# First layer norm: the normalisation moved from VectorE to ScalarE, one tile in each of four steps

## The chip, the cores and the metric

One core of a Trainium2 chip. The metric is the device time of the kernel in microseconds (us), median of the runs shown.

## What is computed

Four sequences of 2048 rows with 256 values each go through an attention and a layer norm, then through a mixture of 32 experts and a second layer norm:

```python
Q, K, V = sign(x * sign(bq)), sign(x * sign(bk)), x * sign(bv)
scores  = einsum('btd,bsd->bts', Q, K) / 16           # causal
x1      = layernorm(x + einsum('bts,bsd->btd', where(causal, sigmoid(4 * scores), 0), V))
probs   = softmax(x1 @ w_router);  top1 = argmax(probs);  gate = probs[top1]
# rows go to the slots of their expert, 320 slots for each; rows over that stay alone
y       = (silu(buf @ w_gate[e]) * (buf @ w_up[e])) @ w_down[e]
out     = layernorm(x1 + gate * y)
```

## The kernel before

The first stage is attention with routing. For each of the four batches b, 40 steps k run over tiles of scores: the rows are taken in four groups g of four tiles (512 rows, GT = 4), and group g takes 4g+4 steps, so that the groups end at steps 3, 11, 23 and 39. The last steps of a group cover 512, 384, 256 and 128 columns. In step k:

- TensorE computes scores(k+2) (L716, L719), then values(k): up to twelve matmuls (L738 to L740), three for each of the four tiles of the group. It is L738 that waits for the two inputs.
- ScalarE computes weights(k): the sigmoid of the scores twice, into a_ring (L572) and, rounded, into the high half of hl_ring (L574). 
- VectorE computes low(k): the difference of the two (L929), the low half of hl_ring. values(k) needs it.

Between these, each engine does the work of the finished groups at steps that tables at the head of the file give. A group's chain is: VectorE adds the residual and takes row statistics (SUM, STATS; L935, L941, L949); GpSimd works out the reciprocal standard deviation with two `pow` operations (rstd, L378 to L388, of which L380 gives the factor that the normalisation needs); VectorE normalises the four tiles into xrow (NORM, L957); TensorE transposes them (TURN, L757), ScalarE copies the transposed rows (COPY, L581), TensorE computes the logits (L765), VectorE picks the expert (L967 to L983), ScalarE computes two sigmoids for the gate (EXPS, L587, L588), VectorE works out the slot and the gate (PLACE, GATE; L1023 is the gate's last operation), and GpSimd scatters the four tiles to the expert buffers with four indirect DMAs (L409). GpSimd also computes rows_alone, the output of rows without an expert, from xrow (L395), and for the next rows the signed values (L357) and their low part (L364). ScalarE computes their high part (VHIGH, L555), the signs (SIGN, L547) and the keys (KEY, L561).

Each engine works through its instructions in the order in which the program lists them: a wait holds up everything behind it on that engine. GpSimd's order within a batch, n being 4b, is rstd and rows_alone of group 3 of the batch before; rstd(n), values_signed(b, 2), values_low(b, 2), rows_alone(n), scatter(n-1), rstd(n+1), values_signed(b, 3), rows_alone(n+1), scatter(n), rstd(n+2), values_low(b, 3), values_signed(b+1, 0), rows_alone(n+2), scatter(n+1), values_low(b+1, 0), values_signed(b+1, 1), scatter(n+2), values_low(b+1, 1). In the first batch there is no group before.

The normalisation of group 3 falls into steps 3 and 4 of the next batch; that of the last batch comes after the loop. The groups' tiles lie in two buffers, res (even groups) and xs (odd groups); xrow has two halves as well, and a half is written again only when the scatter of the group before in it has landed. The second stage, the experts, follows the first and isn't touched by the change.

Of the kernel before, what the change touches and what calls it, by code (L numbers as in the profile page):

```python
# [17 lines left out]
ALU = mybir.AluOpType  # L18
ACT = mybir.ActivationFunctionType
# [12 lines left out]
GT = 4  # L32
# [7 lines left out]
SUM = {0: (2, 3, 4, 4), 1: (10, 11, 12, 12), 2: (22, 23, 24, 24),  # L40
       3: (38, 39, 40, 40)}
STATS = {3: 1, 0: 6, 1: 15, 2: 26}
NORM = {3: (3, 4), 0: (13, 13), 1: (21, 21), 2: (29, 29)}
TURN = {3: 4, 0: 13, 1: 21, 2: 29}
COPY = {3: 6, 0: 15, 1: 23, 2: 31}
ROUTE = {3: 6, 0: 15, 1: 23, 2: 31}
# [13 lines left out]
def bass_postln_attn_moe_kernel(nc, x, bv_q, bv_k, bv_v, w_router, w_gate, w_up, w_down, out):  # L60
    B, T, D = x.shape
    E, _, F = w_gate.shape
    NT = B * T // P
    NG = T // GQ
# [21 lines left out]
    with ExitStack() as ctx:  # L86
# [15 lines left out]
        mone = sb("mone", [P, GT], F32)  # L102
# [16 lines left out]
        mv = sb("mv", [P, GT, 2], F32)  # L119
        small = sb("small", [P, 8, GT], F32)  # L120
        xrow = sb("xrow", [P, 2, GT, ROW], F32)
# [33 lines left out]
        res = (res_even, res_odd)  # L155
# [31 lines left out]
        mv_ready = sem("mv_ready")  # L187
        rstd_step = sem("rstd_step")
        x1_ready = sem("x1_ready")
# [17 lines left out]
        scattered = [sem(f"scattered{i}") for i in range(2)]  # L207
# [23 lines left out]
        def atleast(eng, s, value, settle=False):  # L231

            if isinstance(value, int) and value <= 0:
                return
            if settle and not isinstance(value, int):
                value = eng.to_reg(value)
                eng.wait_ge(consts, 10)
            eng.wait_ge(s, value)  # L240

        block = ctx.enter_context(nc.Block())
        M0, M1 = 6, 7

        def cols(k):
# [78 lines left out]
        def _(pool):  # L324
            g_ = nc.gpsimd
# [38 lines left out]
                g_.tensor_tensor(v_hl[:, 1, sl, :], v_f32, v_hl[:, 0, sl, :].bitcast(F32), ALU.subtract)\  # L364
                    .then_inc(v_ready, 1)

            RN = 6

            def rstd(G, par):


                atleast(pool, mv_ready, (G + 1) * GT, settle=True)

                atleast(pool, alone_ready, G, settle=True)
                base = G * RN
                atleast(pool, x1_ready, G * GT, settle=True)
                var = mv[:, :, 1]
                g_.tensor_scalar(small[:, 0, :], var, EPS, None, ALU.add).then_inc(rstd_step, 1)  # L378
                atleast(pool, rstd_step, base + 1, settle=True)
                g_.tensor_tensor(small[:, 1, :], small[:, 0, :], mhalf[:, :], ALU.pow).then_inc(rstd_step, 1)  # L380
                atleast(pool, rstd_step, base + 2, settle=True)
                g_.tensor_tensor(small[:, 2, :], var, small[:, 1, :], ALU.mult).then_inc(rstd_step, 1)
                atleast(pool, rstd_step, base + 3, settle=True)
                g_.tensor_tensor(small[:, 3, :], small[:, 2, :], small[:, 1, :], ALU.mult).then_inc(rstd_step, 1)
                atleast(pool, rstd_step, base + 4, settle=True)
                g_.tensor_scalar(small[:, 4, :], small[:, 3, :], EPS / 4, None, ALU.add).then_inc(rstd_step, 1)
                atleast(pool, rstd_step, base + 5, settle=True)
                g_.tensor_tensor(small[:, 5, :], small[:, 4, :], mhalf[:, :], ALU.pow).then_inc(rstd_step, 1)  # L388

            def rows_alone(G, half, par):  # L390
# [141 lines left out]
        def _(act):  # L532
            s_ = nc.scalar
# [43 lines left out]
            def copy_x1t(G):  # L577
                act.wait_ge(x1_turned, G + 1)
                atleast(act, logits_done, G)
                for c in range(DC):  # L580
                    s_.activation(x1_t[:, c, :], ps[:, M0 + c, :], ACT.Copy).then_inc(x1t_ready, 1)  # L581

            def gates(G):

                act.wait_ge(below_ready, G + 1)
                atleast(act, gate_ready, G)
                s_.activation(sg[:, 0, :, :], below[:, :, :], ACT.Sigmoid).then_inc(sg_ready, 1)  # L587
                s_.activation(sg[:, 1, :, :], below[:, :, :], ACT.Sigmoid, scale=-1.0).then_inc(sg_ready, 1)  # L588
# [10 lines left out]
            def batch(b, first, last):  # L599
                for k in range(NS):  # L600
                    weights(b, k)
                    for g in (3, 0, 1, 2):
                        if g == 3 and first:
                            continue
                        bb = b - 1 if g == 3 else b
                        if k == COPY[g]:
                            copy_x1t(bb * NG + g)
                        if k == EXPS[g]:
                            gates(bb * NG + g)
                    if first and k == 3:  # L610
                        values_high(0, 1)
                    for q in range(NG):
                        for c in range(DC):
                            if k == KEY[q][c] and not (q == 0 and last):
                                keys(b + 1 if q == 0 else b, q, c)
                        if q in AHEAD and last:
                            continue
                        bb = b + 1 if q in AHEAD else b
                        if k == SIGN[q]:
                            signs(bb, q)  # L620
                        if k == VHIGH[q]:
                            values_high(bb, q)
                    if last and k in (NS - 4, NS - 2):

                        act.wait_ge(pv_done, (B - 1) * NS + OFF[3] + 2 * GT)
                        high_weights(0, (k - NS + 4) // 2)
# [8 lines left out]
            with act.Fori(1, B - 1) as b:  # L635
                batch(b, False, False)
            batch(B - 1, False, True)
            copy_x1t(B * NG - 1)
            gates(B * NG - 1)
            act.wait_ge(table_ready, 1)  # L640
# [265 lines left out]
        def _(dve):  # L906
            v_ = nc.vector
# [24 lines left out]
            def residual(G, i, done, par):  # L932

                dve.wait_ge(pv_done, done)
                v_.tensor_tensor(res[par][:, i, :], ps[:, 2 + i, 0:D], xall[:, G * GT + i, :], ALU.add)\  # L935
                    .then_inc(res_ready, 1)

# [5 lines left out]
            def statistics(G, par):  # L943

                row_statistics(G, GT - 1, par)
                dve.wait_ge(stats_step, (G + 1) * GT)
                atleast(dve, rstd_step, G * 6, settle=True)
                for i in range(GT):
                    v_.bn_aggr(mv[:, i, :], stats[:, par, i, :]).then_inc(mv_ready, 1)  # L949

            def normalise(G, turn, par, tiles=range(GT)):
                dve.wait_ge(rstd_step, G * 6 + 2)
                dve.wait_ge(mv_ready, (G + 1) * GT)

                atleast(dve, scattered[par], turn * 16 * GT)
                for i in tiles:
                    v_.tensor_scalar(xrow[:, par, i, 0:D], res[par][:, i, :], mv[:, i, 0:1], small[:, 1, i:i + 1],  # L957
                                     ALU.subtract, ALU.mult).then_inc(x1_ready, 1)

            SN = 13  # L960

# [75 lines left out]
            def batch(b, first, last):  # L1037
                for k in range(NS):
                    low(b, k)
                    for g in range(NG):  # L1040
                        for i in range(GT):
                            if k == SUM[g][i]:
                                add_tile(b, g, i)
                            if k + NS == SUM[g][i] and not first:
                                add_tile(b - 1, g, i)
                    for g in (3, 0, 1, 2):
                        if g == 3 and first:
                            continue
                        G = (b - 1 if g == 3 else b) * NG + g
                        turn = 2 * b + {3: -1, 0: 0, 1: 0, 2: 1}[g]  # L1050
                        if k == STATS[g]:
                            statistics(G, g % 2)
                        for half in range(2):
                            if k == NORM[g][half]:
                                normalise(G, turn, g % 2, range(half * GT // 2, (half + 1) * GT // 2))
                        if k in (PICK[g], PICK[g] + 1):
                            pick(G, k - PICK[g])
                        if k == PLACE[g]:
                            place(G, g % 2)
                        for part in range(2):  # L1060
                            if k == GATE[g][part]:
                                gate(G, g % 2, part)
                    for q in range(NG):
                        if k == QUERY[q] and not (q in AHEAD and last):
                            queries(b + 1 if q in AHEAD else b, q)
# [11 lines left out]
            G = B * NG - 1  # L1077
# [1 line left out]
            add_tile(B - 1, 3, 3)  # L1079
            statistics(G, 1)  # L1080
            low_weights(0, 0)
            normalise(G, 2 * B - 1, 1)
            low_weights(0, 1)
            pick(G, 0)
            pick(G, 1)
# [97 lines left out]
```

## Time and profile before

| | |
|---|---|
| median of 3 runs | 687.56 us (684.07 to 689.95) |
| span of the profiled execution, first to last instruction | 678.2 us |
| first stage in it | to about 400 us |
| TensorE matmul busy | 604.2 us, 89% |
| mean granted TensorE clock | 0.965 |

Where the engines are in each batch, from the timeline (us; a step's number in brackets):

| batch | weights(3) ends | L380 of group 3 ends | weights(18) ends | L380 of group 1 ends | weights(28) ends | L380 of group 2 ends |
|---|---|---|---|---|---|---|
| 0 | | | 51.25 | 47.59 | 71.41 | 72.63 |
| 1 | 107.09 | 110.57 | 145.52 | 149.80 | 166.02 | 167.24 |
| 2 | 204.16 | 206.81 | 241.66 | 245.95 | 262.16 | 263.45 |
| 3 | 297.43 | 300.86 | 334.65 | 338.76 | 354.72 | 355.52 |

An undisturbed full step, from the start of values(k) to that of values(k+1), takes TensorE 1.87 us, the eight transposes of a group 0.87 us more.

The profile shows for each engine when an instruction ran and what ended the idle time before it. A matmul's record is longer than the distance to the next one, since matmuls are pipelined.

### The profile page before, as it was taken

The page shows a single profiled execution, that of the slowest core. Times are in us where ns is not written, and L with a number is a line of the kernel's source. Part 1 is how long each engine was busy: PE and PEld are TensorE (multiplying, and loading weights), DVE is VectorE, ACT ScalarE, POOL GpSimd, SP SyncE. Part 2 cuts the span into 40 slices and gives each one's busy share as a digit, 9 for nine tenths or more (in the row PEclk, how much of TensorE's full clock was granted, in tenths as well). Part 3 has the DMA queues.
Part 4 walks back from the last instruction along what each step waited for, and adds up shares of the span by engine and source line. Part 5 has one row for each costly group of instructions (what it writes and reads, how often), then busy time and mean ns, then how long its engine had stood idle before and what let it go on. Part 6 is the DMA issues. An engine that isn't in the chain of part 4 may idle for free.

```text
span 678.2 us, 14737 instructions
## 1 busy us (share of the span) xinstructions
PE 604.2 (89%) x4175; PEld 504.3 (74%) x4214; DVE 485.0 (72%) x1300; ACT 353.4 (52%) x678; POOL 415.3 (61%) x547
## 2 busy tenths in 40 slices
PE   5989898899879898988999879999999999999960
PEld 4878787698768687876888637877788778878750
DVE  2669978879787989698898624666776677766740
ACT  5566566456455655666555312555445554555520
POOL 4563757467857377765576520566666666676773
PEclk9999999999999899899999998999999999999995
DMA  8962021132201112206111020566555565566300
GB/s 273 368 211 78 32 80 59 37 96 94 94 29 62 50 39 93 86 23 219 58 59 49 31 87 28 148 193 187 169 158 176 171 190 168 159 184 195 118 32 21
DMA packets 68206, 78.11 MB, mean 115 GB/s; under 512 B 7934, under 2 KB 59374, under 8 KB 68160
## 3 DMA queue, kind: packets, MB, share of 16 engines
q1 hardware_dynamic: 60992, 63.26, 30.1%
q0 software_dynamic: 7168, 14.30, 5.9%
q8 instruction: 21, 0.34, 0.2%
q14 instruction: 25, 0.20, 0.1%
HBM read 44.29 MB, written 37.90 MB: 121 GB/s over the span
## 4 chain that ended last, share of the span: by engine, by line
PE 68%; DVE 9%; issue 8%; ACT 6%; POOL 5%; DMA 2%; SPq 0%; ACTq 0%; DVEq 0%; POOLq 0%
PE ps L877 13%; PE ps L738 8%; PE ps L739 6%; PE ps L740 6%; PE ps L862 6%; PE ps L864 5%; PE ps L863 5%; PE ps L716 5%; PE ps L846 5%; PE ps L765 4%; DVE hl_ring L929 4%; DVE xrow L957 2%; PE ps L757 2%; ACT hl_ring L574 2%; POOL out_dram L490 2%
## 5 line engine op out<-in xcount | busy, mean ns | idle before, releaser
L738 PE MATMUL ps<-v_hl,hl_ring 128*128 128x256 f32 x544 | 176.6, 325 | 25.6 <-DVE hl_ring L929 16.7
L739 PE MATMUL ps<-v_hl,hl_ring 128*128 128x256 f32 x544 | 156.0, 287 | 0.0
L740 PE MATMUL ps<-v_hl,hl_ring 128*128 128x256 f32 x544 | 155.6, 286 | 0.0
L738 PEld LDWEIGHTS ps<-v_hl,hl_ring 128*128 128x128 f32 x544 | 105.9, 195 | 51.5 <-issue 28.4
L490 POOL DMA_INDIRECT out_dram<-alone,ids x96 | 108.0, 1125 | 55.8 <-ACT alone L665 22.5
L572 ACT ACTIVATE a_ring<-ps 128x512 f32<-128x512 f32 (+3 forms) x160 | 85.7, 535 | 91.1 <-PE ps L716 49.9
L929 DVE TENSOR_TENSOR hl_ring<-a_ring,hl_ring 128x512 fp32r<-128x512 f32 (+3 forms) x160 | 119.1, 748 | 19.0 <-ACT hl_ring L574 8.8
L409 POOL DMA_INDIRECT expert_rows<-xrow,slot x64 | 68.7, 1074 | 63.9 <-issue 26.1
L739 PEld LDWEIGHTS ps<-v_hl,hl_ring 128*128 128x128 f32 x544 | 106.2, 195 | 1.9
L740 PEld LDWEIGHTS ps<-v_hl,hl_ring 128*128 128x128 f32 x544 | 106.0, 195 | 0.0
L877 PE MATMUL ps<-xall,a_ring 128*128 128x256 f32 (+1 forms) x384 | 95.9, 392 | 1.1 <-DVE a_ring L1107 1.1
L574 ACT ACTIVATE hl_ring<-ps 128x512 fp32r<-128x512 f32 (+3 forms) x160 | 85.9, 537 | 0.0
L862 PE MATMUL ps<-hl_ring,v_hl 128*128 128x320 f32 x256 | 83.3, 325 | 0.0
L716 PE MATMUL ps<-q_t,k_t 128*128 128x512 bf16 (+3 forms) x284 | 79.9, 354 | 3.3 <-ACT hl_ring L574 1.3
L656 ACT ACTIVATE a_ring<-ps 128x320 f32<-128x320 f32 x64 | 28.0, 437 | 103.8 <-PE ps L864 103.8
L864 PE MATMUL ps<-hl_ring,v_hl 128*128 128x320 f32 x256 | 79.4, 310 | 0.0
L863 PE MATMUL ps<-hl_ring,v_hl 128*128 128x320 f32 x256 | 79.3, 310 | 0.0
L877 PEld LDWEIGHTS ps<-xall,a_ring 128*128 128x128 f32 (+1 forms) x384 | 60.9, 171 | 24.0 <-issue 10.6
L1107 DVE TENSOR_TENSOR a_ring<-a_ring,ps 128x320 f32<-128x320 f32 x64 | 31.2, 488 | 56.4 <-ACT a_ring L656 56.4
L395 POOL TENSOR_TENSOR alone<-xrow,small 128x1024 f32<-128x1024 f32 x16 | 33.8, 2112 | 42.2 <-DVE xrow L957 31.9
L862 PEld LDWEIGHTS ps<-hl_ring,v_hl 128*128 128x128 f32 x256 | 48.4, 189 | 12.4 <-issue 12.2
L665 ACT ACTIVATE alone<-z,zrs 128x256 f32<-128x256 f32 (+1 forms) x96 | 50.3, 588 | 9.4 <-POOL zrs L481 9.4
(108 smaller groups left out, 1125.3 us busy)
## 6 DMA issues: line engine op xcount, KB each, us to landing
expert_rows<-xs SPq DMA_DIRECT2D x40, 258.0 KB, 5.6
xs<-expert_rows SPq DMA_DIRECT2D x32, 258.0 KB, 3.0
xall<-in_L_attn_x_dram SPq DMA_DIRECT2D x16, 512.0 KB, 4.1
out_dram<-alone SPq DMA_DIRECT2D x16, 512.0 KB, 3.1
xall<-in_L_ffn_w_gate_dram SPq DMA_DIRECT2D x32, 256.0 KB, 3.6
xall<-in_L_ffn_w_up_dram SPq DMA_DIRECT2D x32, 256.0 KB, 3.9
xall<-in_L_ffn_w_down_dram SPq DMA_DIRECT2D x32, 256.0 KB, 4.2
xs<-expert_rows SPq DMA_DIRECT2D x32, 64.5 KB, 3.0
```

What stands on the lines that cost most here:

```text
L490: g_.indirect_dma_start(out=out_rows, out_offset=bass.IndirectOffsetOnAxis(ap=ids[0:rows, n % U, t:t + 1], axis=0), in_=o_s[0:rows, p, t, ...
L572: s_.activation(a_ring[:, r, lo:GQ], ps[:, k % 2, lo:GQ], ACT.Sigmoid, scale=0.25)\
L574: s_.activation(hl_ring[:, 0, r, lo:GQ], ps[:, k % 2, lo:GQ], ACT.Sigmoid, scale=0.25)\
L716: last = mm(o, k_t[:, c, j * P:(j + 1) * P], q_t[:, c, g * GQ + lo:(g + 1) * GQ], start=(c == 0), stop=(c == DC - 1 and not diag))
L738: mm(o, ah, v_hl[:, 0, j, :], start=(j == 0), stop=False)
L739: mm(o, ah, v_hl[:, 1, j, :], start=False, stop=False)
L740: last = mm(o, al, v_hl[:, 0, j, :], start=False, stop=(j == GT * g + i))
L862: mm(o, wh, x_h[:, p, c, :], start=(c == 0), stop=False)
L863: mm(o, wh, x_l[:, p, c, :], start=False, stop=False)
L864: last = mm(o, wl, x_h[:, p, c, :], start=False, stop=(c == DC - 1))
L877: last = mm(o, act_h[:, p, f, t * P:t * P + m], raw[:, s, 4 + f, :], start=(f == 0), stop=(f == FC - 1))
L929: v_.tensor_tensor(hl_ring[:, 1, r, lo:GQ], a_ring[:, r, lo:GQ], hl_ring[:, 0, r, lo:GQ].bitcast(F32), ALU.subtract).then_inc(al_ready, 1)
```

## The change

- The four VectorE operations (L957) that subtract the mean and multiply by the reciprocal standard deviation are gone. ScalarE computes `scale * x + bias` instead, with bias = -mean * rstd.
- For that GpSimd's rstd has two more operations: -mean, ahead of the first pow, and its product with rstd, behind it. A group has now eight steps of `rstd_step` (RN = 8), and the normalisation waits for the fourth, where it waited for the second.
- NORM gives a step for each tile. ScalarE does a tile's normalisation right behind weights(k), ahead of its other work of that step. Group 0 begins at step 10 (before: 13), group 1 at 18 (21), group 2 at 28 (29), group 3 at 3 (3).
- residual waits for the normalisation two groups before, whose buffer it writes (it was VectorE's own order before).

```diff
-NORM = {3: (3, 4), 0: (13, 13), 1: (21, 21), 2: (29, 29)}
+NORM = {3: (3, 3, 4, 4), 0: (10, 11, 12, 13), 1: (18, 19, 20, 21), 2: (28, 28, 29, 29)}
@@ rstd, GpSimd
                 g_.tensor_scalar(small[:, 0, :], var, EPS, None, ALU.add).then_inc(rstd_step, 1)
-                atleast(pool, rstd_step, base + 1, settle=True)
+                g_.tensor_tensor(small[:, 6, :], mv[:, :, 0], mone[:, :], ALU.mult).then_inc(rstd_step, 1)
+                atleast(pool, rstd_step, base + 2, settle=True)
                 g_.tensor_tensor(small[:, 1, :], small[:, 0, :], mhalf[:, :], ALU.pow).then_inc(rstd_step, 1)
-                atleast(pool, rstd_step, base + 2, settle=True)
+                atleast(pool, rstd_step, base + 3, settle=True)
+                g_.tensor_tensor(small[:, 7, :], small[:, 6, :], small[:, 1, :], ALU.mult).then_inc(rstd_step, 1)
@@ ScalarE
+            def normalise(G, turn, par, tiles=range(GT)):
+                act.wait_ge(rstd_step, G * RN + 4)
+                atleast(act, scattered[par], turn * 16 * GT)
+                for i in tiles:
+                    s_.activation(xrow[:, par, i, 0:D], res[par][:, i, :], ACT.Identity,
+                                  bias=small[:, 7, i:i + 1], scale=small[:, 1, i:i + 1]).then_inc(x1_ready, 1)
@@ ScalarE, batch, behind weights(b, k)
+                        for i in range(GT):
+                            if k == NORM[g][i]:
+                                normalise(bb * NG + g, turn, g % 2, range(i, i + 1))
@@ VectorE, residual
                 dve.wait_ge(pv_done, done)
+                atleast(dve, x1_ready, (G - 1) * GT)
@@ VectorE
-            def normalise(G, turn, par, tiles=range(GT)):
-                dve.wait_ge(rstd_step, G * 6 + 2)
-                dve.wait_ge(mv_ready, (G + 1) * GT)
-                atleast(dve, scattered[par], turn * 16 * GT)
-                for i in tiles:
-                    v_.tensor_scalar(xrow[:, par, i, 0:D], res[par][:, i, :], mv[:, i, 0:1], small[:, 1, i:i + 1],
-                                     ALU.subtract, ALU.mult).then_inc(x1_ready, 1)
```

## Rows read from the trace of the kernel before

**Rows 1.** Groups by line and shape (busy, mean, idle before), then L957 alone (min/median/max).

```profile
L957 DVE TENSOR_SCALAR xrow<-res,mv,small 128x256 f32<-128x256 f32 x32 | 25.8, 866 | 0.0
L957 DVE TENSOR_SCALAR xrow<-xs,mv,small 128x256 f32<-128x256 f32 x32 | 17.6, 604 | 1.9 <-POOL small L380 1.9
L957 DVE TENSOR_SCALAR xrow<-res,mv,small x32: 399/407/2593, 41.0 to 361.0; 128x256 f32<-128x256 f32 x32
```

**Rows 2.** Waits of TensorE, 22 to 400 us: total, times, longest.

```profile
PE ps L738 <- DVE hl_ring L929: 15.4, 19, 2.0
PE ps L757 <- DVE xrow L957: 7.5, 4, 2.0
```

**Rows 3.** Timeline of batch 1 around step 18: start, duration, idle before.

```profile
144.93 0.59 ACT L574 ACTIVATE hl_ring<-ps 128x512 fp32r<-128x512 f32 x1
146.53 0.31 ACT L587 ACTIVATE sg<-below 128x128 f32<-128x128 f32 x1 [1.01 <-DVE below L974]
146.63 1.33 POOL L409 DMA_INDIRECT expert_rows<-xrow,slot  x1 [0.30 <-issue]
146.95 0.58 ACT L572 ACTIVATE a_ring<-ps 128x512 f32<-128x512 f32 x1
148.52 1.28 POOL L380 TENSOR_TENSOR small<-small,mhalf 128x4 f32<-128x4 f32 x1
150.24 0.36 PE L738 MATMUL ps<-v_hl,hl_ring 128*128 128x256 f32 x1
```

**Rows 4.** Timeline: three ScalarE affine operations and one small GpSimd one, second stage.

```profile
504.06 1.57 ACT L665 ACTIVATE alone<-z,zrs 128x256 f32<-128x256 f32 x3
479.77 0.20 POOL L481 TENSOR_TENSOR zrs<-zrs 128x3 f32<-128x3 f32 x1
```

**Rows 5.** Timeline of batch 2, steps 3 and 4.

```profile
203.89 0.27 ACT L574 ACTIVATE hl_ring<-ps 128x128 fp32r<-128x128 f32 x1
206.97 0.73 DVE L957 TENSOR_SCALAR xrow<-xs,mv,small 128x256 f32<-128x256 f32 x2 [0.42 <-POOL small L380]
208.54 0.38 PE L738 MATMUL ps<-v_hl,hl_ring 128*128 128x256 f32 x1 [0.60 <-DVE hl_ring L929]
```

**Rows 6.** Timeline of batch 1, steps 28 to 30.

```profile
165.43 0.59 ACT L574 ACTIVATE hl_ring<-ps 128x512 fp32r<-128x512 f32 x1
166.20 1.04 POOL L380 TENSOR_TENSOR small<-small,mhalf 128x4 f32<-128x4 f32 x1
167.16 0.60 ACT L572 ACTIVATE a_ring<-ps 128x512 f32<-128x512 f32 x1 [0.20 <-PE ps L716]
169.56 5.48 DVE L957 TENSOR_SCALAR xrow<-res,mv,small 128x256 f32<-128x256 f32 x4
169.80 2.41 POOL L364 TENSOR_TENSOR v_hl<-z,v_hl 128x1024 fp32r<-128x1024 f32 x1
172.46 2.42 POOL L357 TENSOR_TENSOR z<-xall,bv_row 128x1024 f32<-128x1024 f32 x1 [0.25 <-POOL v_hl L364]
175.09 0.44 PE L757 MATMUL ps<-ident,xrow 128*128 128x128 f32 x2 [1.91 <-DVE xrow L957]
175.78 0.36 PE L738 MATMUL ps<-v_hl,hl_ring 128*128 128x256 f32 x1
```

**Rows 7.** Timeline of batch 1, steps 10 and 11.

```profile
126.81 2.36 POOL L364 TENSOR_TENSOR v_hl<-z,v_hl 128x1024 fp32r<-128x1024 f32 x1 [2.33 <-ACT v_hl L555]
127.08 2.24 DVE L929 TENSOR_TENSOR hl_ring<-a_ring,hl_ring 128x128 fp32r<-128x128 f32 x1
```

**Rows 8.** Busy time by window (us, instructions): PE, PEld, DVE, ACT, POOL; granted clock, DMA.

```profile
130.00:132.00 2.00, 0.51 (x3) 0.01 (x1) 1.93 (x9) 2.00 (x4) 0.00 (x0) 1.00 0.00 0
132.00:134.00 2.00, 1.91 (x11) 1.92 (x12) 2.00 (x6) 0.07 (x1) 0.00 (x0) 0.65 0.00 0
134.00:136.00 2.00, 2.00 (x9) 1.54 (x9) 2.00 (x6) 0.47 (x1) 0.64 (x1) 0.50 0.00 0
```

**Rows 9.** Timeline of the end of the first stage.

```profile
384.14 1.38 DVE L957 TENSOR_SCALAR xrow<-xs,mv,small 128x256 f32<-128x256 f32 x4 [1.24 <-POOL small L380]
386.06 1.08 ACT L581 ACTIVATE x_t<-ps 128x512 f32<-128x512 f32 x2 [7.82 <-PE ps L757]
```

More of the change, by code:

```diff
@@ L242, in bass_postln_attn_moe_kernel @@
         block = ctx.enter_context(nc.Block())
+        RN = 8
         M0, M1 = 6, 7
@@ L365, in values_low @@
                     .then_inc(v_ready, 1)
-            RN = 6
             def rstd(G, par):
@@ L378, in rstd @@
                 g_.tensor_scalar(small[:, 0, :], var, EPS, None, ALU.add).then_inc(rstd_step, 1)
-                atleast(pool, rstd_step, base + 1, settle=True)
+                g_.tensor_tensor(small[:, 6, :], mv[:, :, 0], mone[:, :], ALU.mult).then_inc(rstd_step, 1)
+                atleast(pool, rstd_step, base + 2, settle=True)
                 g_.tensor_tensor(small[:, 1, :], small[:, 0, :], mhalf[:, :], ALU.pow).then_inc(rstd_step, 1)
-                atleast(pool, rstd_step, base + 2, settle=True)
+                atleast(pool, rstd_step, base + 3, settle=True)
+                g_.tensor_tensor(small[:, 7, :], small[:, 6, :], small[:, 1, :], ALU.mult).then_inc(rstd_step, 1)
                 g_.tensor_tensor(small[:, 2, :], var, small[:, 1, :], ALU.mult).then_inc(rstd_step, 1)
-                atleast(pool, rstd_step, base + 3, settle=True)
+                atleast(pool, rstd_step, base + 5, settle=True)
                 g_.tensor_tensor(small[:, 3, :], small[:, 2, :], small[:, 1, :], ALU.mult).then_inc(rstd_step, 1)
-                atleast(pool, rstd_step, base + 4, settle=True)
+                atleast(pool, rstd_step, base + 6, settle=True)
                 g_.tensor_scalar(small[:, 4, :], small[:, 3, :], EPS / 4, None, ALU.add).then_inc(rstd_step, 1)
-                atleast(pool, rstd_step, base + 5, settle=True)
+                atleast(pool, rstd_step, base + 7, settle=True)
                 g_.tensor_tensor(small[:, 5, :], small[:, 4, :], mhalf[:, :], ALU.pow).then_inc(rstd_step, 1)
@@ L605, in batch @@
                         bb = b - 1 if g == 3 else b
+                        turn = 2 * b + {3: -1, 0: 0, 1: 0, 2: 1}[g]
+                        for i in range(GT):
+                            if k == NORM[g][i]:
+                                normalise(bb * NG + g, turn, g % 2, range(i, i + 1))
                         if k == COPY[g]:
@@ L637, in _ @@
             batch(B - 1, False, True)
+            normalise(B * NG - 1, 2 * B - 1, 1)
             copy_x1t(B * NG - 1)
@@ L946, in statistics @@
                 dve.wait_ge(stats_step, (G + 1) * GT)
-                atleast(dve, rstd_step, G * 6, settle=True)
+                atleast(dve, rstd_step, G * RN, settle=True)
                 for i in range(GT):
                     v_.bn_aggr(mv[:, i, :], stats[:, par, i, :]).then_inc(mv_ready, 1)
-            def normalise(G, turn, par, tiles=range(GT)):
-                dve.wait_ge(rstd_step, G * 6 + 2)
-                dve.wait_ge(mv_ready, (G + 1) * GT)
-                atleast(dve, scattered[par], turn * 16 * GT)
-                for i in tiles:
-                    v_.tensor_scalar(xrow[:, par, i, 0:D], res[par][:, i, :], mv[:, i, 0:1], small[:, 1, i:i + 1],
-                                     ALU.subtract, ALU.mult).then_inc(x1_ready, 1)
             SN = 13
@@ L1049, in batch @@
                         G = (b - 1 if g == 3 else b) * NG + g
-                        turn = 2 * b + {3: -1, 0: 0, 1: 0, 2: 1}[g]
                         if k == STATS[g]:
                             statistics(G, g % 2)
-                        for half in range(2):
-                            if k == NORM[g][half]:
-                                normalise(G, turn, g % 2, range(half * GT // 2, (half + 1) * GT // 2))
                         if k in (PICK[g], PICK[g] + 1):
@@ L1081, in _ @@
             low_weights(0, 0)
-            normalise(G, 2 * B - 1, 1)
             low_weights(0, 1)
```

## The prediction

> **What bounds the kernel now.** Only the first stage, to about 400 us, is touched. I read the waits of TensorE in it first, then the groups of instructions by line, then the timeline step by step, noting for each of the 160 steps when weights, low and values started.
>
> TensorE is the bound where it isn't waiting, and most of its waits end with a VectorE operation: 15.4 us for the low halves and 7.5 us, four times about 1.9, for the normalised rows [rows 2]. The normalisation takes 43.4 us of VectorE though one operation, undisturbed, takes 0.407 us, or 26.0 us for 64; the 17.4 us above that are blocking [rows 1]. The reader sees it at step 29: the four operations take 5.48 us while GpSimd runs L364 and L357 under them, TensorE waits 1.91 us, and values(30) starts at 175.78, where 1.87 for values(29) and 0.87 for the transposes behind its start at 170.52 would give about 173.3 [rows 6]. So VectorE looks overloaded, and ScalarE idle for long times. But the wait that I looked for next is another: when is the factor ready that the normalisation needs, and where is ScalarE then in its own program?
>
> **What is removed.** 43.4 us of VectorE, 26.0 of them work. On TensorE's path that is at most the 7.5 us.
>
> **What is added on ScalarE.** 64 affine operations with a scale and a bias for each row. The same shape and form runs in the second stage: three in 1.57 us [rows 4], one alone 0.59, so each further one costs (1.57 - 0.59) / 2 = 0.49 us of the engine, 31 us in all, 1.96 for a group. ScalarE is some 0.8 us idle in a full step of 1.87 us, so the work alone fits. Its bound is 0.49 from below and 0.59 from above; I take 0.49, since they stand in a queue of others.
>
> **What is added on GpSimd.** Two small operations, 0.20 us each by the nearest row [rows 4], the second behind a semaphore: L380 ends, and 0.14 us later the next begins. The factor and the bias are there 0.25 + 0.35 = 0.6 us later than the pow's end in before. From below it is 0.4 (no gap), from above 0.9 (L382 takes up to 0.44).
>
> **The wait, group by group.** On ScalarE it holds back weights of the next steps, which low and then values wait for.
>
> *Group 1, steps 18 to 21.* In batch 1, weights(18) ends at 145.52. The factor comes from L380, which ends at 149.80, since it stands in GpSimd's order behind the scatter of four tiles, whose last starts at 146.63, and that waits for a gate of step 16 [rows 3]. With the 0.6 us ScalarE stands still till 150.4, 4.9 us, where VectorE came to this only at 152.34. Then: one tile 0.49, the gates 0.42 (146.53 to 146.95), weights(19) 1.06, low 0.69 and 0.2 for the semaphores: values(19) starts at 153.3, for 150.24 [rows 3]. That is 3.0 us of TensorE. Steps 20 and 21 carry a tile and a key each (0.49 + 0.72 + 0.96 = 2.2 us for a step of 1.87), 0.3 us more; some 0.3 us of waiting at steps 22 and 23, where GpSimd's L395 blocks low, goes away. Sum 3.0 us. Batches 2 and 3 repeat it (weights(18) ends 241.66 and 334.65, L380 at 245.95 and 338.76); in batch 0 there is no scatter ahead, and the factor is early. 3 x 3.0 = 9.0 us. The scatter into this half of xrow must also have landed; a landing takes 2.7 us from 146.63 to 147.96, so it comes at 149.3 to 150.7, with the factor.
>
> *Group 3, steps 3 and 4 of the next batch.* In batch 2, weights(3) ends at 204.16. The factor came at 206.81, VectorE waited for it too (0.42) and needed 0.73 for two tiles; values(4) started at 208.54 [rows 5]. Now ScalarE waits till 207.4, does two tiles (208.4) and only then weights(4), which was done at 207.10 before: 209.5, low 210.2, values(4) 210.3. That is 1.8 us; ScalarE then has two tiles and a key before weights(5) and two more operations before weights(6), and with rows_alone blocking low(5) I get 2.2 at values(5) and 2.0 at values(6). Batches 1 and 3 look the same (ScalarE would wait 4.1 and 4.0 us). 3 x 2.0 = 6.0 us.
>
> *Group 2, steps 28 and 29.* Weights(28) ends at 166.02, the factor is there at 167.24 + 0.6 = 167.85, a wait of 1.8 us (the same in all four batches, 1.4 to 1.9). Two tiles and the signs (1.0) move the start of weights(29) from 167.16 [rows 6] to 169.8, its end to 170.8. By then L364, 0.45 us later for the two new operations, runs from 170.3 to 172.7, then L357 [rows 6]. The question is whether low, which takes the place of the normalisation on VectorE, is blocked as it was. It is an operation on two tiles in SBUF, and at step 11 one of 0.28 us takes 2.24 us under L364, whose end it waits for [rows 7]. So low(29) runs at 172.7, low(30) at 175.7, values(30) starts at 176.5, for 175.78: the stall isn't taken away but moved, and 0.7 us are lost. Batch 0 gives 0.3, batch 3 between 0 and 2.1, taken as 1. Sum 2.7 us.
>
> The Trainium skill says in "SBUF — State Buffer", Who interferes with whom, that a VectorE instruction with two SBUF inputs contends with a GpSimd instruction that reads SBUF, and not only the two-port modes do. By a reading in which only the two-port modes block, the three stalls of about 2.5 us at step 30 would go and the sum would be some 8 us lower; the trace agrees with the page's wider rule, by the 2.24 us.
>
> *Group 0, steps 10 to 13.* The factor is early. A tile ahead of L555 moves L364, which waits for it, by 0.49 us, and with it the end of the blocked low(11) [rows 7]: 0.5 us in batches 1 to 3, 1.5 us. The 1.4 us that VectorE saves at step 13 are given to no wait: TensorE has none behind it.
>
> *The end.* Behind the last batch nothing covers the chain. VectorE's four tiles start at 384.14 and take 1.38; ScalarE starts 0.6 later and takes 3 x 0.49 + 0.59 = 2.06; the copies at 386.06 [rows 9] move by up to 1.3 us. TensorE transposes tile by tile: 1.0 us.
>
> The new wait of residual costs nothing: the group two before was normalised at least 17 steps earlier.
>
> **Sum.** 9.0 + 6.0 + 2.7 + 1.5 + 1.0 = 20.2 us on a span of 678.2. The median of the runs is 687.6, 9.4 above the span, and I carry the difference over: 707.8, rounded to 708 us.
>
> **The rivals.**
>
> *More: the clock.* After waits of 1.3, 1.6 us and others in the same few us, TensorE's granted clock is 0.65 and then 0.50, its lower level of 1.2 GHz, from about 132.6 to 136 us [rows 8]; five such stretches of 3.4 us lie in the first stage, each worth 1.7 us. One wait of 1.9 us by itself, at 175, brought none. Each of my six stalls of 2 to 3 us could bring one: 6 x 1.7 = 10 us, 718 us. For it: the stalls of 2.0 us at 200 and at 80 did. Against it: the stalls at 174 didn't, and some of the five old ones may go.
>
> *About the same: the delay is given back.* VectorE has 26 us less to do, and the 15.4 us of waits for low [rows 2] are partly its own queue at steps 0 to 12 and 34. If 12 of them went, the sum would be 8 us, 696; with an earlier factor (scatter shorter, GpSimd ahead) it would be within 1%. Against it: most of these waits end when a GpSimd operation ends, as at step 11 [rows 7], and that order isn't changed. About 690.
>
> *Faster: the relief counts.* ScalarE's waits are covered and VectorE's 7.5 us for the rows go, with two of the stretches at the lower clock (3.4 us): 687.6 - 10.9 = 677 us. It decides at step 18: weights(19) must start by 148.3, so the factor must be there by 147.4, 3 us earlier than the rows give it [rows 3]. The Trainium skill says in "Perfetto Trace Analysis", Optimizing Scalar/DVE Operations, that offloading work to ScalarE may make sense where VectorE is saturated; VectorE's share here bears that out, the order of the waits doesn't.
>
> **How the numbers follow.** The forecast 0.60, more by the clock 0.18, given back 0.13, faster 0.09. Slower by over 1% is then 0.78, within 1% 0.12, faster 0.10; 1%, 6.9 us, is about what a measurement of this kernel can tell from no change. The range leaves out the faster case and the half of the third that lies lowest: from 692 (a third of the sum left) to 718 (the clock in full).
>
> **What would show it.** In the profile after: ScalarE's operation on xrow waits for GpSimd's small tile, some 3 to 5 us, six times, at steps 3 and 18; waits of TensorE for ScalarE's or VectorE's hl_ring grow by 15 to 20 us and those for xrow vanish; low operations of 2 to 3 us appear at steps 29 and 30. I am wrong if ScalarE's waits for the small tile stay below 10 us in all, or if they are there and TensorE's idle time in the first stage doesn't grow.

## The result: 4% slower, and the profile after

| | before | after |
|---|---|---|
| median of 5 runs each | 687.83 us (684.07 to 693.30) | 717.38 us (711.29 to 718.86) |
| ratio, 95% interval | | 1.0399 [1.034, 1.0458] |
| again, beside the experiments | 689.37 us (13 runs) | 714.37 us (4 runs), 1.0365 [1.0295, 1.0434] |
| span of the profiled execution | 678.2 us | 709.5 us |
| mean granted TensorE clock in it | 0.965 | 0.959 |

Ratios, here and below, compare the faster executions of each kernel with each other; medians are over all of them. The forecast was 708 us, from 692 to 718: slower, and the time is in the range, 0.6 us from its upper end. The change costs 29.5 us between the medians and 31.3 us between the spans, where 20.2 us were forecast.

First the engines' busy time in the profile of after:

```profile
PE 610.3 (86%) x4175; PEld 508.6 (72%) x4214; DVE 459.4 (65%) x1236; ACT 382.3 (54%) x742; POOL 416.9 (59%) x579
```

VectorE is busy 25.6 us less than before (485.0 there), ScalarE 28.9 us more (353.4 there). The work went where it was sent, ScalarE is still idle almost half of the time, and the kernel is slower: shares of busy time say nothing here. The waits do. TensorE's and ScalarE's in the first stage of after, 22 to 425 us (total, times, longest):

```profile
PE ps L752 <- DVE hl_ring L943: 30.5, 32, 2.2
PE ps L730 <- ACT hl_ring L575: 16.9, 10, 3.6
PE ps L752 <- ACT hl_ring L575: 6.0, 5, 1.3
PE ps L771 <- ACT xrow L589: 3.3, 1, 3.3
```

```profile
ACT xrow L589 <- POOL small L382: 39.6, 11, 7.3
```

The second fence is the cause, as the experiments below bear out, the first its effect. ScalarE's normalisation (L589) waits for GpSimd's bias (L382) eleven times. One of them, 7.3 us, is at the end of the stage, where ScalarE has nothing else to do; the ten others are 32.3 us in the middle of the loop. TensorE waits 30.5 us for low (L943; the answering row was 15.4 us in [rows 2]) and 22.9 us for ScalarE's weights (8.4 us in before), most of it in front of the next scores (L730), since ScalarE hadn't read the old ones. Together these waits grew by 29.6 us, for the 15 to 20 us that the forecast named. The four waits for xrow of [rows 2], 7.5 us, are down to the one at the end.

The timeline of batch 1 around step 18, answering to [rows 3] (start, duration, idle before):

```profile
151.64 0.59 ACT L575 ACTIVATE hl_ring<-ps 128x512 fp32r<-128x512 f32 x1
153.24 0.31 ACT L596 ACTIVATE sg<-below 128x128 f32<-128x128 f32 x1 [1.00 <-DVE below L981]
153.65 1.01 POOL L410 DMA_INDIRECT expert_rows<-xrow,slot  x1 [0.30 <-issue]
155.40 1.04 POOL L380 TENSOR_TENSOR small<-small,mhalf 128x4 f32<-128x4 f32 x1
156.59 0.20 POOL L382 TENSOR_TENSOR small<-small 128x4 f32<-128x4 f32 x1
156.82 0.60 ACT L589 ACTIVATE xrow<-xs,small 128x256 f32<-128x256 f32 x1 [3.07 <-POOL small L382]
157.33 0.58 ACT L573 ACTIVATE a_ring<-ps 128x512 f32<-128x512 f32 x1
158.48 0.69 DVE L943 TENSOR_TENSOR hl_ring<-a_ring,hl_ring 128x512 fp32r<-128x512 f32 x1 [3.46 <-ACT hl_ring L575]
158.82 2.59 POOL L358 TENSOR_TENSOR z<-xall,bv_row 128x1024 f32<-128x1024 f32 x1
160.07 1.49 DVE L1022 TENSOR_TENSOR quot<-quot,sg 128x128 f32<-128x128 f32 x1
161.48 0.68 DVE L943 TENSOR_TENSOR hl_ring<-a_ring,hl_ring 128x512 fp32r<-128x512 f32 x1
163.12 1.89 POOL L396 TENSOR_TENSOR alone<-xrow,small 128x1024 f32<-128x1024 f32 x1 [1.71 <-ACT xrow L589]
163.13 1.90 DVE L1013 SCALAR_TENSOR_TENSOR slot<-rt 128x4 uint32<-128x4 f32 x1
164.96 0.88 DVE L943 TENSOR_TENSOR hl_ring<-a_ring,hl_ring 128x384 fp32r<-128x384 f32 x2
```

Weights(18) ends at 152.23. The gates (L596, L597) come at 153.24 to 153.75, and then ScalarE stands still until L382 ends at 156.79: the factor is 4.56 us behind weights(18). Weights(19), the next line of the program, can't start before 157.33, and low(19) waits for it on an idle VectorE (3.46 us). So far that is the forecast. The second half of the fence is not in it: GpSimd's L358 and L396 now lie over small operations of the gate on VectorE, L1022 (1.49 us) and L1013 (1.90 us), and low(20) and low(21) stand behind these.

Group 2, batch 1, steps 28 to 30, answering to [rows 6]:

```profile
177.81 0.53 POOL L377 TENSOR_SCALAR small<-mv 128x4 f32<-128x4 f32 x1 [4.98 <-issue]
180.24 1.10 ACT L589 ACTIVATE xrow<-res,small 128x256 f32<-128x256 f32 x2 [2.81 <-POOL small L382]
182.16 2.35 POOL L365 TENSOR_TENSOR v_hl<-z,v_hl 128x1024 fp32r<-128x1024 f32 x1
182.19 0.57 ACT L573 ACTIVATE a_ring<-ps 128x512 f32<-128x512 f32 x1
183.34 1.72 DVE L943 TENSOR_TENSOR hl_ring<-a_ring,hl_ring 128x512 fp32r<-128x512 f32 x1 [2.16 <-ACT hl_ring L575]
184.76 2.54 POOL L358 TENSOR_TENSOR z<-xall,bv_row 128x1024 f32<-128x1024 f32 x1 [0.25 <-POOL v_hl L365]
185.29 2.56 DVE L943 TENSOR_TENSOR hl_ring<-a_ring,hl_ring 128x512 fp32r<-128x512 f32 x1 [0.23 <-ACT hl_ring L575]
```

ScalarE waits again, 2.81 us. Low(29) and low(30), 0.69 us when undisturbed, take 1.72 and 2.56 us under L365 and L358; each ends 0.55 us behind the end of the GpSimd operation over it. The blocking that the normalisation suffered in [rows 6] has moved onto low. Over the whole stage VectorE's group of low shows it (busy, mean ns, idle before and its releasers); before, this group was busy 115.2 us, mean 742 ns:

```profile
L943 DVE TENSOR_TENSOR hl_ring<-a_ring,hl_ring 128x512 fp32r<-128x512 f32 (+3 forms) x156 | 127.2, 820 | 73.0 <-ACT a_ring L573 38.2 <-ACT hl_ring L575 31.8 <-issue 1.7
```

Low is busy 12.0 us longer for the same 156 operations; in before the normalisation was blocked for 17.4 us.

**Where the 31.3 us lie.** From the start of values at the ends of the stretches, after minus before, summed over the batches (where four numbers follow, they are batches 0 to 3):

| stretch of steps | group at work | forecast | measured |
|---|---|---|---|
| 34 of the batch before to 9 (step 3) | 3 | 6.0 | 7.8 |
| 9 to 18 (step 10) | 0 | 1.5 | 0.5 |
| 18 to 25 (step 18) | 1 | 9.0 | 12.05: 0, 4.04, 4.02, 4.00 |
| 25 to 34 (step 28) | 2 | 2.7 | 9.6: 4.66, 1.48, 1.49, 1.96 |
| end of the stage | 3 of the last batch | 1.0 | 1.4 |

### The profile page after: what moved, and what is told of

Read it like the earlier page. It is cut to its first block, busy times and chain, and to the rows that moved or that the text cites. A ratio compares the mean times of both kernels' runs of the same rounds, so it can differ in the third digit from the quotient of the medians.

```text
span 709.5 us, 14839 instructions
## 1 busy us (share of the span) xinstructions
PE 610.3 (86%) x4175; PEld 508.6 (72%) x4214; DVE 459.4 (65%) x1236; ACT 382.3 (54%) x742; POOL 416.9 (59%) x579
## 4 chain that ended last, share of the span: by engine, by line
PE 52%; issue 15%; ACT 10%; DVE 10%; POOL 9%; DMA 1%; ACTq 1%; POOLq 0%; DVEq 0%; SPq 0%
PE ps L891 12%; PE ps L876 6%; DVE hl_ring L943 6%; PE ps L878 5%; PE ps L877 5%; PE ps L860 5%; PE ps L752 4%; PE ps L754 3%; PE ps L753 3%; POOL expert_rows L410 3%; ACT a_ring L573 3%; PE ps L779 3%; ACT hl_ring L575 2%; PE ps L730 2%; PE ps L771 2%
## 5 line engine op out<-in xcount | busy, mean ns | idle before, releaser
L943 DVE TENSOR_TENSOR hl_ring<-a_ring,hl_ring 128x512 fp32r<-128x512 f32 (+3 forms) x160 | 131.1, 824 | 73.0 <-ACT a_ring L573 38.2
L410 POOL DMA_INDIRECT expert_rows<-xrow,slot x64 | 66.8, 1044 | 88.2 <-issue 47.8
L730 PE MATMUL ps<-q_t,k_t 128*128 128x512 bf16 (+3 forms) x284 | 80.5, 356 | 21.0 <-ACT hl_ring L575 17.3
L396 POOL TENSOR_TENSOR alone<-xrow,small 128x1024 f32<-128x1024 f32 x16 | 32.7, 2042 | 28.6 <-ACT xrow L589 22.7
```

The source lines that it names most:

```text
L730: last = mm(o, k_t[:, c, j * P:(j + 1) * P], q_t[:, c, g * GQ + lo:(g + 1) * GQ], start=(c == 0), stop=(c == DC - 1 and not diag))
L943: v_.tensor_tensor(hl_ring[:, 1, r, lo:GQ], a_ring[:, r, lo:GQ], hl_ring[:, 0, r, lo:GQ].bitcast(F32), ALU.subtract).then_inc(al_ready, 1)
```

## The experiments

The theory: the price is ScalarE standing still in its own order for a factor that GpSimd has ready only later. The rivals: the 31 us of added work on ScalarE; the two added operations on GpSimd; the clock. A difference from one experiment to the next is read together with the granted clock, since the kernel before alone runs from 681.5 to 699.4 us, most of it with its clock. "Clock-free" is a rough correction: the median of time minus span x (1 - granted clock) over all executions, this kernel minus before on the same chip. A single execution of before lies some 2.3 us around its median by this measure. It can take off too much: in after, batch 1 has a stretch at the lower clock behind step 18 and batch 2 has none, and both lose the same 4.0 us there.

| run | median / before | ratio [95%] | clock-free |
|---|---|---|---|
| e1_waits_only | 696.60 / 691.16 | 1.0128 [1.007, 1.0185] | +7.1 |
| e2_work_only | 695.63 / 691.16 | 1.005 [1.0011, 1.009] | +1.3 |
| e3_pool_only | 684.91 / 691.16 | 0.9919 [0.9886, 0.9953] | -0.9 |
| e4_g1_late | 704.12 / 691.16 | 1.0151 [1.0064, 1.0239] | +12.7 |
| e5_wait_and_work | 700.14 / 689.37 | 1.0181 [1.0119, 1.0242] | +10.5 |
| e6_all_late | 690.26 / 689.37 | 1.0026 [0.9992, 1.006] | +3.1 |
| e7_g0_only | 693.88 / 689.37 | 1.0109 [1.0029, 1.0188] | -0.2 |
| after_again | 714.37 / 689.37 | 1.0365 [1.0295, 1.0434] | +23.9 |
| e8_g2_late_only | 682.85 / 690.30 | 0.992 [0.9886, 0.9953] | -4.3 |
| e9_wait_work_pool | 712.32 / 690.30 | 1.0334 [1.0286, 1.0382] | +12.0 |

**e1: the waits alone.** The kernel before, ScalarE waits for the factor and does nothing with it:

```diff
+            HOLD = {3: 3, 1: 18, 2: 28}
+                        if k == HOLD.get(g):
+                            act.wait_ge(rstd_step, (bb * NG + g) * 6 + 2)
```

> The kernel before, VectorE normalises as it did; ScalarE does no new work, but waits at steps 3, 18 and 28, where the changed kernel's normalisation begins, for GpSimd's factor of that group. Theory of the wait (what costs is that ScalarE's queue stands still until GpSimd has the factor, 4.6 us at step 18 in the trace after): 12 to 22 us slower than before. Rival of the work (what costs is 64 times 0.49 us on ScalarE, 31 us, which happens to be the whole difference): the same as before, within 3 us.

A wait that guards nothing costs 1.3%, 7.1 us without the clock: more than the rival's 3 us, less than the 12 to 22 us expected. In its profile ScalarE waits 10.3 + 3.6 us for GpSimd's factor, and the steps 17 to 25 of batch 1 take 18.86 us, where they take 16.76 in before and 20.80 in after. So the wait is a cause, about a third of the whole by this run (its factor comes from before's shorter chain).

**e2: the work alone.** The kernel before, with ScalarE operations of the same shape and number at the new steps, without a wait. Their rows are extra work that nobody reads.

```diff
+EXTRA = {3: (3, 3, 4, 4), 0: (10, 11, 12, 13), 1: (18, 19, 20, 21), 2: (28, 28, 29, 29)}
+                        for i in range(GT):
+                            if k == EXTRA[g][i]:
+                                s_.activation(idle[:, i, :], bv_row[:, :], ACT.Identity, bias=mone[:, i:i + 1],
+                                              scale=mhalf[:, i:i + 1])
```

> The kernel before, VectorE normalises as it did; ScalarE does at each of the new steps one affine operation of the same shape and form, from a constant row into a tile that nobody reads, without a wait. Theory of the wait: 1 to 8 us slower than before, since a full step leaves ScalarE 0.8 us. Rival of the work: 25 to 31 us slower.

0.5%, 1.3 us of it left without the clock, for 64 operations that take 31 us of the engine. That is in the 1 to 8 us expected. The rival of the work falls: ScalarE had the room.

**e3: the two GpSimd operations alone.** Before with after's rstd; VectorE waits for step 4 of rstd_step and normalises as it did.

> The kernel before with GpSimd's two new small operations of each group, and VectorE's normalisation waits for the second of them. ScalarE has nothing new. Theory of the wait: 0 to 3 us slower, 0.45 us in each of the places where GpSimd is late. A rival, that GpSimd's longer chain is what delays everything behind it: 7 us (16 times 0.45) or more.

Not slower, as 0 to 3 us had been expected, but 0.8% faster: 6.3 us between the medians, of which the clock-free time leaves 0.9 us. The longer chain costs nothing where ScalarE doesn't stand waiting for it. Why the clock was higher in this kernel (median 0.963, before 0.956) isn't shown.

**e4: group 1 three steps later.** The kernel after, with one entry changed:

```diff
-NORM = {3: (3, 3, 4, 4), 0: (10, 11, 12, 13), 1: (18, 19, 20, 21), 2: (28, 28, 29, 29)}
+NORM = {3: (3, 3, 4, 4), 0: (10, 11, 12, 13), 1: (21, 21, 22, 22), 2: (28, 28, 29, 29)}
```

> The changed kernel with one number pattern changed: group 1 is normalised at steps 21, 21, 22, 22 instead of 18, 19, 20, 21, when the factor is there. Theory of the wait: of the 12 us that the trace after shows between steps 18 and 25 some 9 to 12 go, 18 to 23 us over before. Rival of the work: nothing changes, 29 us over before, or more since two tiles stand in one step.

The ratio falls from 1.0365 to 1.0151, the clock-free loss from 23.9 to 12.7 us (13.0 us between the medians, less than the 18 to 23 expected). In its profile ScalarE waits eight times for L382, where it waited eleven times, and the stretch of steps 18 to 25 loses 2.65 us, for 12.05. The work and where it is done are after's; the place of one group in ScalarE's program alone is worth 11 us, clock-free. Its waits:

```profile
ACT xrow L589 <- POOL small L382: 28.1, 8, 7.3
```

**e5: wait and work.** e2, with ScalarE waiting for before's factor in front of its first extra operation of a group (the extra rows are again read by nobody).

> Both halves together in the kernel before: ScalarE waits for GpSimd's factor at the first step of each group and does one affine operation in each of the four places, on rows that nobody reads; VectorE still normalises. If wait and work were priced apart, the sum of the two runs before this: 9 + 3 = 12 us slower than before. If they multiply (what the wait leaves behind, a queue with no slack, meets a step that is 0.2 us too long for ScalarE), 20 to 30 us, and nothing of the change's price has to do with VectorE.

1.0181, against 1.0128 and 1.005 for the two alone: they add up, as the first of the two expectations had it, and make not quite half of the clock-free loss of after (10.5 of 23.9 us).

**e6: everything late.** The kernel after, with each group at a step where its factor is ready; for group 0 that is where it was:

```diff
-NORM = {3: (3, 3, 4, 4), 0: (10, 11, 12, 13), 1: (18, 19, 20, 21), 2: (28, 28, 29, 29)}
+NORM = {3: (5, 5, 6, 6), 0: (10, 11, 12, 13), 1: (21, 21, 22, 22), 2: (29, 29, 30, 30)}
-TURN = {3: 4, 0: 13, 1: 21, 2: 29}
+TURN = {3: 5, 0: 13, 1: 22, 2: 30}
```

> The changed kernel with ScalarE's normalisation at steps at which the factor is there: group 3 at 5, 5, 6, 6, group 1 at 21, 21, 22, 22, group 2 at 29, 29, 30, 30, and the transposes of these groups one step later (5, 22, 30). Theory of the wait: at most 10 us over before, since work alone cost 3 and the end 1. Rival of the work: 25 us or more. If 12 to 20 us, late rows cost what the early wait did.

1.0026: nearly the whole loss is gone, with all 64 tiles on ScalarE and the two operations on GpSimd. ScalarE's waits in its profile, of which 7.3 us are the harmless one at the end:

```profile
ACT xrow L589 <- POOL small L382: 8.7, 4, 7.3
```

And its steps 29 and 30 of batch 1:

```profile
174.12 1.09 ACT L589 ACTIVATE xrow<-res,small 128x256 f32<-128x256 f32 x2 [0.61 <-POOL small L382]
175.12 0.58 ACT L573 ACTIVATE a_ring<-ps 128x512 f32<-128x512 f32 x1
176.05 2.39 POOL L365 TENSOR_TENSOR v_hl<-z,v_hl 128x1024 fp32r<-128x1024 f32 x1
176.27 2.72 DVE L943 TENSOR_TENSOR hl_ring<-a_ring,hl_ring 128x512 fp32r<-128x512 f32 x1 [0.47 <-ACT hl_ring L575]
178.69 2.54 POOL L358 TENSOR_TENSOR z<-xall,bv_row 128x1024 f32<-128x1024 f32 x1 [0.25 <-POOL v_hl L365]
179.43 1.82 DVE L1030 TENSOR_SCALAR xrow<-rt 128x4 f32<-128x4 f32 x1
```

Low(29) is through before L365 starts; only low(30) is blocked (2.72 us), and under L358 lies no low but the gate's last operation. Steps 25 to 34 take 21.91 us, where they take 25.14 in before and 26.62 in after.

**e7: group 0 alone on ScalarE**, at steps 10 to 13; the other groups on VectorE as before, with after's rstd (VectorE waits for its third step).

> Only group 0, whose factor is early, is normalised on ScalarE at steps 10 to 13; groups 1, 2 and 3 are normalised on VectorE at the steps of before. Theory of the wait: within 3 us of before, a quarter of the work is moved and none of the waits. Rival of the work: a quarter of 30 us, 7 us slower. If moving work off VectorE helps where nothing waits, faster by up to 3 us.

Slower by 1.1% with an interval from 0.3 to 1.9%, over four executions, and nothing of it left without the clock (-0.2 us). By the ratio alone the rival's 7 us would fit, by the clock-free time it wouldn't: inconclusive.

**e8: group 2 alone, late.** Only group 2 on ScalarE, at steps 29, 29, 30, 30, with TURN[2] = 30; the others on VectorE as in e7.

> Only group 2 is normalised on ScalarE, at steps 29, 29, 30, 30, with its transposes at step 30; groups 0, 1 and 3 stay on VectorE at the steps of before. In the run in which all groups were late, values(34) came 3.2 to 3.9 us earlier across group 2 in three batches, and later elsewhere. Theory of the wait: where the factor is there, taking the four blocked operations off VectorE is a gain, 3 x 3.3 = 10 us, against up to 4 us for GpSimd's two operations: 3 to 10 us faster than before. Rival, that low takes the place of the normalisation behind the same GpSimd operations (the step of the prediction): the same as before, within 3 us.

0.992 [0.9886, 0.9953], clock-free -4.3 us, the lowest median of all kernels (682.85 us, 12 runs). It beats both kernels, before by 0.8%. Steps 25 to 34 take 21.30 us in batches 1 and 2 each, for 25.14 and 25.21 in before. This is the relief of VectorE that the change could bring. Some of it is given back at once: in batches 1 and 2 another small operation of VectorE, L997, is through only when the next long one of GpSimd is (L365, 189.74 to 192.12): 3.20 us for 0.29. TensorE waits for it, and steps 34 to 40 take 1.9 and 1.6 us more than in before.

```profile
189.08 3.20 DVE L997 TENSOR_TENSOR hot<-iota_e,topf 128x128 bf16<-128x128 f32 x1
192.34 0.19 PE L788 MATMUL ps<-hot,tri 128*128 128x32 bf16 x1 [1.64 <-DVE hot L997]
```

e3 reaches the same ratio without moving any work. Of its 6.3 us the clock-free time leaves 0.9, of e8's 7.5 us 4.3, so a part of e8's gain is the clock too (median 0.966, before 0.958).

**e9: wait and work, with the longer GpSimd chain.** e5 on after's rstd; ScalarE waits for step 4 (the extra rows are again read by nobody).

> As the run with wait and work together (VectorE still normalises, ScalarE's operations write rows that nobody reads), and GpSimd's rstd is that of the changed kernel, with its two more operations, whose end ScalarE waits for. If the rest of the difference between that run (11 to 12 us) and the changed kernel (25 us) comes from the longer chain on GpSimd: 20 to 25 us slower than before. If it comes from what depends on the rows being made on ScalarE (transposes, rows without an expert and the scatter behind them): 12 to 15 us.

1.0334, for 1.0181 in e5: the same two operations that were free in e3 count under ScalarE's waits, which are these:

```profile
ACT idle L614 <- POOL small L385: 25.9, 10, 4.5
```

By its medians it loses 22.0 us, in the 20 to 25 us expected if the rest of after's price is the longer chain, and its interval overlaps that of after (25.0 us beside the experiments). A large part of that is the clock (median 0.943, before 0.958 on that chip; in the first stage of its profile 25.6 us go to the clock, 13.6 in after): clock-free it loses 12.0 us, only 1.5 more than e5, and after 23.9. So between 3 us (with the clock) and 12 us (without it) of after are in none of its parts as long as VectorE makes the rows. Which of the two is nearer stays open.

## Why the prediction was right, and where its sizes were off

**The mechanism** was the forecast's, but that the time lies in the range is in part luck. The sum was 20.2 us and 31.3 came; the room above 708 had been left for the clock. The clock brought at most 5 us of the excess, and the rest, 6 us or more, are terms of the sum that were too small, group 2's above all. What the price hangs on is the place of the wait in ScalarE's order: e1 (the wait alone costs), e2 (the work alone costs little), e4 and e6 (later steps take the loss away) show it. Of the signs named, ScalarE's waits for the small tile came in all six places, 2.9 to 4.3 us for 3 to 5; they are 32.3 us outside the end, far above the 10 that would have refuted it.

**Group 1, step 18: 9.0 forecast, 12.05 measured.** The factor came 4.56 us behind weights(18), for 4.9. The forecast put the gates behind the tile; the program has them ahead, where VectorE's L981 made ScalarE wait 1.00 us anyway. So from values(18) to values(19) it lost 2.4 us, for 3.0. The step that failed is the next one, 0.3 us for steps 20 and 21, 2.9 us as it turned out: values(21) is 5.3 us behind before's pace from values(18). ScalarE's own step was near the forecast, 2.06 us between its last two weights for 2.2; what was missing is VectorE. L358 starts right behind the factor's chain, at 158.82, and L396 when ScalarE's fourth tile is there; with ScalarE late, L1022 and L1013 of the gate fall under them (undisturbed 0.29 and 0.16 us; in after L1022 takes 1.49 us and L1013 1.90, 1.89 and 1.75 us in batches 1, 2 and 3; in before neither is blocked at these steps) and low(20) and low(21) stand behind them. 1.2 us is given back by step 25. The first of these blockings needs only the wait: L1022's counterpart takes 1.82 us in e1 and 1.49 us in e5 and e9. The second comes, in these runs, only when the rows are made on ScalarE; in after because L396 then starts behind ScalarE's fourth tile. In e9 the slot's operation keeps its 0.16 us:

```profile
166.52 1.49 DVE L1025 TENSOR_TENSOR quot<-quot,sg 128x128 f32<-128x128 f32 x1
169.59 0.16 DVE L1016 SCALAR_TENSOR_TENSOR slot<-rt 128x4 uint32<-128x4 f32 x1
```

Steps 18 to 25 lose 8.2 us in e9 and 12.05 in after, and L1013 is a candidate for these 4 us. I read it in the timelines, and no run changed it by itself, so it isn't shown.

**Group 2, step 28: 2.7 forecast, 9.6 measured.** In batch 0 it lost 4.66, for 0.3: the factor was late there for a reason outside the forecast (next section), and ScalarE waited 4.54 us, for 1.8. In batches 1 to 3 the chain began late too: the waits were 2.81, 2.81 and 2.22. The low halves did take 1.72 and 2.56 us, as named. A third piece, 0.9 us in batch 1 between values(25) and values(27), goes with a wait of ScalarE that has no releaser in the kernel (next section).

The forecast said of this group that the stall isn't taken away but moved. That holds only for the early wait, which makes low(29) late enough to meet L365. With two tiles behind weights(29) and two behind weights(30), e6 and e8 gain 3.2 to 3.9 us a batch in batches 1 and 2, before they give back 1.6 to 2.0 us by step 40. The faster rival was therefore wrong of this change and right of a neighbour of it, and only e6 and e8 could tell.

On this blocking the Trainium skill says in "SBUF — State Buffer", Who interferes with whom, that a VectorE instruction with two SBUF inputs contends with GpSimd reading SBUF. The trace agrees for low: 2.56 us under L358, for 0.69. The gate's L1022 agrees too, 1.49 for 0.29 us. L1030, which reads one tile, was blocked as well, 1.82 us in e6; that row isn't explained by two inputs.

**Group 3: 6.0 forecast, 7.8 measured**, waits of 4.30, 3.38 and 3.17 us for 4.1, 3.2 and 4.0. The mechanism and, within a third, the size hold; 3.4 of the 7.8 us are time at the lower clock in batches 1 and 3, where before has none. **Group 0: 1.5 forecast, 0.5 measured**; e7 doesn't settle it. **The end: 1.0 forecast, 1.4 measured.**

**The clock**, the rival with 10 us more: the time lost to it in the first stage, summed over windows of 1 us, is 13.6 us in after and 8.5 in before, so it brought at most 5 us, half of what the rival gave it. These 5 us are part of the 31.3 in the table of stretches, whose forecasts left the clock out. Three of its stretches in batch 1 (us, busy time of PE, PEld, DVE, ACT, POOL; granted clock, DMA):

```profile
112.00:115.00 3.00, 3.00 (x15) 2.54 (x14) 2.07 (x9) 0.00 (x0) 1.76 (x5) 0.53 0.00 0
139.00:142.00 3.00, 3.00 (x15) 2.54 (x15) 3.00 (x6) 1.25 (x3) 2.61 (x3) 0.59 0.12 43
160.00:163.00 3.00, 2.92 (x15) 2.42 (x14) 2.97 (x9) 3.00 (x8) 1.41 (x1) 0.50 0.00 0
```

The last lies right behind the stall at step 18; before had one stretch in this batch, at 132 [rows 8]. That last one cost nothing: values(19) to values(25) are as late in batch 2, where the clock was full.

**Given back:** only the 1.2 us above. VectorE's lighter load shortened no wait as long as ScalarE was late: TensorE's waits for low doubled.

## What to carry to other kernels

An engine that works in program order pays for an operation at the step where it stands, from that step until its last input is ready, with everything behind it; so ask first when the input is ready on the other engine's timeline, and place the operation behind that moment, not where the engine looks idle. A stall of one engine also shifts the others against each other: look which small operations come to lie under a long one that blocks them. When an offload loses, move it by a step or three before giving it up: the same 64 operations cost 3.7% early and 0.3% late, and one quarter of them, alone and late, gained 0.8%, of which a part is the clock.

## What the runs showed of the hardware that I hadn't expected

**GpSimd's first scatter.** In batch 0 the first scatter operation starts 0.96 us behind the copy of the token numbers in before, and 5.63 us behind what is ahead of it in after:

```profile
64.28 1.24 POOL L409 DMA_INDIRECT expert_rows<-xrow,slot  x1 [0.96 <-POOL tok L401]
```

```profile
67.53 1.24 POOL L410 DMA_INDIRECT expert_rows<-xrow,slot  x1 [5.63 <-issue]
```

The profile names nothing that it waits for. It is 0.96 us in e1, e2 and e5, which have the old rstd, and 3.8 to 5.6 us in e3, e4, e6, e7, e8, e9 and both runs of after, which have the two more operations. Ahead of the factor of group 2 in batch 0 in GpSimd's order, it delays that too. The profile's queue of instructions moved 31 packets in after, e4 and e6, but 25 or 26 in before and in e3, e7, e8 and e9, so this count doesn't go with the wait; the cause stays open.

**A wait at the same step of the loop.** At step 26 of batches 1 and 2 ScalarE waits 1.84 and 1.89 us for something that the profile calls remote, once each; in before there is none, in e4 and e6 there are waits of 0.9 to 1.0 us at other steps. Its cause stays open:

```profile
173.70 0.60 ACT L573 ACTIVATE a_ring<-ps 128x512 f32<-128x512 f32 x1 [1.84 <-remote]
```

**The clock sets much of the spread.** Of two executions of before on one chip, the one with a granted clock of 0.952 had a span of 691.6 us, the one with 0.972 of 680.5 us. A difference of 1% between two kernels of this kind can be mostly the clock, as e3 and e7 suggest with opposite signs.
